# Stage 4 of a four-stage transformer kernel: comparisons in two parts, turned tiles ahead of sparse rows, weight roundings on other engines and steps

## The chip, the cores and the metric

The kernel runs on one core of a Trainium2 chip. The metric is the device time of one execution in microseconds (us), the median of the runs shown. In the profile PE is TensorE, PEld its weight loads, DVE VectorE, ACT ScalarE, POOL GpSimd and SP SyncE, which issues the DMAs. L686 is line 686 of the kernel. PSUM has eight banks of 512 float32 a partition.

## What is computed

Four residual blocks on x (2 x 1024 rows of 512, float32): each adds the layer norm of a block applied to the layer norm of x. The blocks are a per-token attention over heads, a feed-forward with ternary weights, a causal attention with rotary positions, and the one that most of the change touches:

```
h = silu(x @ w_gate) * (x @ w_up)          # 512 -> 2048
g = h.reshape(B, S, I // 4, 4)
_, idx = top_k(abs(g), 2)                  # of each four neighbours the two largest stay
h_sparse = g where kept, else 0
x = x + layernorm(h_sparse @ w_down)       # 2048 -> 512
```

## The kernel before

**Stages.** Stages 1 to 3 are the first three blocks. Stage 3 ends with `attention()`, a loop of 384 score units n on every engine: TensorE computes scores, ScalarE takes the exponential (L1349), GpSimd masks the diagonal (L1703), TensorE weighs the values two steps later. Then 12 steps `project(step)` follow, which project the second batch's eight tiles: ScalarE makes the high half of a tile (`out_hi`, tile OT, L1166), VectorE the low half (`out_lo`, L686), TensorE multiplies; statistics go over VectorE, GpSimd (L1588, L1594) and ScalarE (`norm6`), and GpSimd adds the residual (`residual`).

**Stage 4.** The rows are taken in four blocks k of 512, and each block in 16 steps, so s runs from 0 to 63, k = s // 16. Step s makes 128 of the 2048 hidden columns, transposed: hidden on partitions, 512 rows along the free axis. The hidden columns are dealt out so that four steps (a group g = s // 4) hold the four neighbours among which two are kept; comparing is then elementwise between four tiles. All products are float32 made of three passes with a rounded high half (float32r) and the low half of each operand, so every operand has to be split: the high half is a rounding copy, the low half a subtraction.

**TensorE** (`gate_up`, L2065): for step s 12 matmuls for gate into one PSUM bank and 12 for up into the next; then `down4(q)` for one hidden tile q of the sparse result, by the list `quarters` (L436): q is taken 7 to 9 steps after it was made, none before step 8. Gate, up and the turned tiles share a ring of four banks (4 to 7): each takes the bank of the fourth one before it in the list `fours` (L2049 `wait4`). So up of step s needs the bank of up of step s - 2, freed by VectorE's product; at steps 14 and 15 of a block, where two turned tiles (`turn4`, L2055) stand ahead of gate and up, up needs that of step s - 1.

**ScalarE**, each step s, in this order: at s % 16 in 13 and 14 two normalizations of the next block's rows (`norm4`), at 14 and 15 the high halves of two turned tiles (`turn4`, tile xT4); silu of gate (tile sl, L1553); then `split_w` three times, the high halves of the weights of gate and up for step s + 3 and down for q = s - 4 (ws_g, ws_u, ws_d, L1166); then `absolute(s)` (L1491, tile ab from hm), which waits for VectorE's product. Only at s % 4 == 3 is the absolute row ahead of the three copies.

**GpSimd**, each step: the low halves of the same weights (L1588). When the fourth of a weight block of four is done, SP issues the DMA that overwrites its slot of `rw4` (1 MB, four slots, asked for about a group ahead). At s % 16 == 6 it makes the statistics of the block before and adds its output rows to xb, at 11 the statistics of the next block's rows.

**VectorE**, each step s, in this order:

```
if g >= 1 and s % 4 == 0: sparse(g - 1, 0)     # compare: six is_ge rows from ab4 into cm4
if k < 3 and s % 16 == 11: four stats(...)     # L702, L703, L692, of the next block's rows
if g >= 1 and s % 4 == 1: sparse(g - 1, 1)     # count: 8 additions on cm4, 4 masks on hm4
if g >= 1 and s % 4 == 2: sparse(g - 1, 2)     # 4 casts to HH4 (L1079), 4 subtractions
if k < 3 and s % 16 in (14, 15): two turn4     # low halves of turned tiles
gate_up(s)                                     # hm4 = PSUM up * silu, frees both banks
```

`sparse(g, 0)` waits for all four absolute rows of its group; `compare` has three instructions, of 1536, 1024 and 512 columns. `absolute` of the next group waits until they are done (semaphore cma). After step 63 `last_compare(part)` and `last_count(part)` treat the last group in two halves of 256 columns, and the down products of the last four hidden tiles follow tile by tile.

**Around attention's end.** At n = 363, 366, 369 and 372 ScalarE rounds the first four gate weights (`split_w("g", ...)`) behind its exponential, GpSimd subtracts at the same n. In `project`, steps 2, 4 and 6, both do so for the first three up weights, behind `out_hi` and `norm6` of the step.

## Time and profile before

| what | us |
| --- | --- |
| median of 3 runs | 1397.03 |
| lowest and highest | 1394.22, 1397.66 |
| the profiled execution's own time | 1397.03 |
| its span in the trace | 1395.3 |
| TensorE busy | 1329.8 |
| VectorE busy | 1038.5 |
| GpSimd busy | 694.1 |
| ScalarE busy | 666.0 |

The trace covers the span; 1.73 us of the execution lie around it. Times in a timeline count from the span's start. A row of a timeline merges neighbouring instructions of one kind: start, time they took together, engine, line, operation, tiles (written <- read), shapes, how many. A bracket at its end is the time for which the engine had been idle, with the instruction that ended the wait. Attention's last units run at about 800 to 820, the projection to 845, stage 4 from there to the end.

### The profile page before, as it was taken

What the parts mean: (1) busy time and instruction counts of PE and PEld (TensorE: products, weight loads), DVE (VectorE), ACT (ScalarE), POOL (GpSimd) and SP (SyncE); (2) the same over time, 40 slices, a digit from 0 to 9 for tenths busy, and PEclk for the clock granted to TensorE, in tenths of its full rate; (3) what the DMA queues carried; (4) which work ended last, traced back from release to release, by engine and by line L of the source; (5) the groups of instructions that cost most, each with busy time, mean ns of one, the idle gap of its engine ahead of it and who ended that gap; (6) DMA issues with size and microseconds to landing.
All of it is one profiled execution on the core that took longest, in us unless ns stands there. A gap on an engine that the chain in (4) does not pass through costs nothing.

```text
span 1395.3 us, 19463 instructions
## 1 busy us (share of the span) xinstructions
PE 1329.8 (95%) x7206; PEld 912.9 (65%) x7206; DVE 1038.5 (74%) x1959; ACT 666.0 (48%) x1153; POOL 694.1 (50%) x836
## 2 busy tenths in 40 slices
PE   6989999999999899999999999998999999999997
PEld 5875446556455454555555467787888788878886
DVE  5898575665857758677666443998889878988897
ACT  6664342232325545455555575445454544454442
POOL 2576241421313413332433366776678768866863
PEclk9999999999999999999999999999999999999999
DMA  9100210204113213123013223122323422322300
GB/s 334 74 1 1 76 61 16 91 1 121 53 46 99 77 25 85 49 70 119 24 54 90 86 92 151 62 98 95 115 86 134 151 108 87 134 112 91 121 31 30
DMA packets 46270, 116.86 MB, mean 84 GB/s; under 512 B 3420, under 2 KB 4448, under 8 KB 42336
## 3 DMA queue, kind: packets, MB, share of 16 engines
q1 hardware_dynamic: 45104, 114.31, 24.0%
q8 instruction: 57, 0.93, 0.3%
q10 hardware_dynamic: 1072, 1.31, 0.3%
q14 instruction: 37, 0.30, 0.1%
HBM read 92.28 MB, written 23.07 MB: 83 GB/s over the span
## 4 chain that ended last, share of the span: by engine, by line
PE 61%; DVE 26%; ACT 5%; POOL 4%; issue 3%; DMA 1%; POOLq 0%; DVEq 0%; ACTq 0%
PE PS L1784 59%; DVE cm L686 7%; DVE SM L702 2%; DVE PS L919 2%; DVE HH L686 2%; DVE hm L695 2%; PE PS L1793 2%; DVE hm L686 1%; DMA rw<-in_L_ffn_w_up 1%; DVE HH L1079 1%; ACT EX L1349 1%; POOL SM L1588 1%; DVE HHx L1079 1%; DVE SM L698 1%; POOL ws_u L1588 1%
## 5 line engine op out<-in xcount | busy, mean ns | idle before, releaser
L1349 ACT ACTIVATE EX<-PS 128x512 f32<-128x512 f32 (+3 forms) x384 | 170.3, 494 | 134.4 <-PE PS L1784 132.6
L1588 POOL TENSOR_TENSOR SM<-SM 128x1 f32<-128x1 f32 x128 | 84.6, 661 | 214.4 <-DVE SM L692 210.6
L919 DVE CUSTOM_DVE_ANT_0 PS<-PS,MW 128x128 f32<-128x128 f32 (+3 forms) x256 | 122.5, 504 | 62.9 <-PE PS L1784 62.6
L1588 POOL TENSOR_TENSOR ws_g<-rw,ws_g 128x512 fp32r<-128x512 f32 x64 | 113.9, 1780 | 92.8 <-ACT ws_g L1166 92.8
L1784 PE MATMUL PS<-KG,QG 96*128 96x512 f32 (+3 forms) x384 | 134.8, 381 | 17.4 <-DVE SM L919 7.5
L1703 POOL TENSOR_SCALAR_AFFINE_SELECT EX<-EX 128x128 f32<-128x128 f32 x256 | 74.7, 302 | 149.0 <-ACT EX L1349 146.5
L1588 POOL TENSOR_TENSOR ws_u<-rw,ws_u 128x512 fp32r<-128x512 f32 x64 | 125.7, 1964 | 34.1 <-ACT ws_u L1166 34.1
L1784 PE MATMUL PS<-QG,KG 98*128 98x512 f32 (+3 forms) x384 | 131.3, 376 | 3.1 <-ACT EX L1349 2.7
L1784 PE MATMUL PS<-ws_d,HH 128*128 128x512 f32 x528 | 125.8, 389 | 0.9 <-DVE HH L686 0.8
L686 DVE TENSOR_TENSOR cm<-cm 128x512 bf16<-128x512 bf16 (+1 forms) x136 | 124.8, 948 | 2.4
L1784 PEld LDWEIGHTS PS<-QG,KG 98*128 98x128 f32 x384 | 69.6, 190 | 71.9 <-issue 45.6
L698 DVE TENSOR_REDUCE SM<-PS 128x1 f32<-128x512 f32 x128 | 87.7, 685 | 36.4 <-PE PS L1784 36.2
L1784 PEld LDWEIGHTS PS<-ws_d,HH 128*128 128x128 f32 x528 | 98.9, 188 | 22.2 <-issue 1.2
L1588 POOL TENSOR_TENSOR ws_d<-rw,ws_d 128x512 fp32r<-128x512 f32 x64 | 101.0, 1579 | 14.3 <-ACT ws_d L1166 14.3
L1784 PEld LDWEIGHTS PS<-KG,QG 96*128 96x128 f32 x384 | 72.2, 190 | 49.9 <-DVE SM L919 20.0
L686 DVE TENSOR_TENSOR cm<-ab 128x512 bf16<-128x512 f32 (+4 forms) x51 | 95.6, 1927 | 11.2 <-ACT ab L1491 11.2
L1784 PE MATMUL PS<-xT4a,ws_u 128*128 128x512 f32 x384 | 94.1, 395 | 4.9 <-DVE hm L686 4.8
L1491 ACT ACTIVATE ab<-hm 128x512 f32<-128x512 f32 x64 | 40.4, 632 | 120.9 <-DVE hm L686 120.9
L1784 PE MATMUL PS<-xT4b,ws_u 128*128 128x512 f32 x384 | 92.5, 390 | 0.8 <-DVE hm L686 0.7
L1784 PE MATMUL PS<-xT4a,ws_g 128*128 128x512 f32 x384 | 92.7, 390 | 0.0
L1784 PE MATMUL PS<-xT4b,ws_g 128*128 128x512 f32 x384 | 92.5, 390 | 0.0
L1166 ACT ACTIVATE ws_u<-rw 128x512 fp32r<-128x512 f32 x64 | 72.2, 1128 | 41.3 <-DMA rw<-in_L_ffn_w_up 41.3
(203 smaller groups left out, 2825.5 us busy)
## 6 DMA issues: line engine op xcount, KB each, us to landing
rw<-in_L_ffn_w_gate SPq DMA_DIRECT2D x16, 1024.0 KB, 5.1
rw<-in_L_ffn_w_up SPq DMA_DIRECT2D x16, 1024.0 KB, 7.1
rw<-in_L_ffn_w_down SPq DMA_DIRECT2D x16, 1024.0 KB, 7.9
QG<-qs SPq DMA_DIRECT2D x48, 256.0 KB, 4.2
raw<-in_L_ffn_w SPq DMA_DIRECT2D x3, 2816.0 KB, 11.6
qs<-stg SPq DMA_DIRECT2D x16, 512.0 KB, 3.5
xA<-xs SPq DMA_DIRECT2D x2, 2048.0 KB, 7.8
ys<-xA SPq DMA_DIRECT2D x4, 1024.0 KB, 4.2
```

Of the source, the lines that this page charges most:

```text
L686: return e.tensor_tensor(out, a, b, op)
L695: return e.scalar_tensor_tensor(out=out, in0=a, scalar=s, in1=b, op0=op0, op1=op1)
L698: return e.tensor_reduce(out, a, AX.X, op)
L702: w.wait_ge(S["dvs"], did(e.bn_stats(st, src)))
L919: last = e.tensor_tensor_reduce(out=p, in0=p, in1=MW[:, 512 - k1 + k0:512], scale=1.0, scalar=BIG, op0=ALU.add, op1=ALU.max, accum_out=m1)
L1079: n = did(e.tensor_copy(sparse4(q, 0), h[:, r, :]))
L1166: return e.activation(out, in_, ACT.Copy, scale=scale, bias=0.0)
L1349: e.activation(EX[:, n % 16, 0:W], PS[:, score_bank(n), 0:W], ACT.Exp, scale=ISQ, bias=0.0).then_inc(S["ex"], 1)
L1491: e.activation(ab4[:, s % 4, :], hm4[:, s // 4 % 2, s % 4, :], ACT.Abs, scale=1.0, bias=0.0).then_inc(S["ab"], 1)
L1588: return e.tensor_tensor(out, a, b, op)
L1703: e.affine_select(out=p, in_=p, compare_op=ALU.is_ge, fill=0.0, base=0, pattern=[[1, 128]], channel_multiplier=-1).then_inc(S["sel"], 1)
L1784: return e.matmul(out, l, r, start=start, stop=stop, skip_group_check=free)
```

## The change

It has five edits.

1. `compare` becomes `compare_three` (three of the six comparisons, those among the first three tiles; two instructions of 1024 and 512 columns) and `compare_last` (those with the fourth tile, one of 1536). `compare_three` of group g runs as `sparse(g, -1)` at s % 4 == 3, ahead of that step's product, and waits for three absolute rows; `compare_last` stays at s % 4 == 0. `last_compare` has only `compare_last` in it. `count` reads the rows in their new order.
2. VectorE makes the low halves of the turned tiles ahead of casts and subtractions, and the four statistics of step 11 two at step 11 and two at step 12 (GpSimd's likewise).
3. ScalarE's `absolute(s)` stands right behind silu in every step.
4. The high halves of the first four gate weights are made by VectorE (`gate_hi`, a `tensor_copy`), at the same n of its own order.
5. The third up weight is split at step 8 of the projection, on ScalarE and GpSimd.

```diff
+            def gate_hi(s):
+                q = raw_no[("g", 0)]
+                w.wait_ge(S["d_r%d" % (q % 4)], 16 * (q // 4 + 1))
+                w.wait_ge(S["st"], 336)
+                src = rw4[:, slot_r(q), :].rearrange("p (c g r) -> p r c g", c=4, r=4)[:, s]
+                e.tensor_copy(ws_g[:, s, 0, :].rearrange("p (c g) -> p c g", c=4), src).then_inc(S["hg"], 1)
...
+                    if n in (363, 366, 369, 372):
+                        gate_hi((n - 363) // 3)
...
-            def compare(a, cm, W):
-                tt(cm[:, 0:3, :], a[:, 0:1, :].broadcast_to([128, 3, W]), a[:, 1:4, :], ALU.is_ge)
-                tt(cm[:, 3:5, :], a[:, 1:2, :].broadcast_to([128, 2, W]), a[:, 2:4, :], ALU.is_ge)
-                return tt(cm[:, 5, :], a[:, 2, :], a[:, 3, :], ALU.is_ge)
+            def compare_three(a, cm, W):
+                tt(cm[:, 0:2, :], a[:, 0:1, :].broadcast_to([128, 2, W]), a[:, 1:3, :], ALU.is_ge)
+                return tt(cm[:, 2, :], a[:, 1, :], a[:, 2, :], ALU.is_ge)
+            def compare_last(a, cm, W):
+                return tt(cm[:, 3:6, :], a[:, 0:3, :], a[:, 3:4, :].broadcast_to([128, 3, W]), ALU.is_ge)
...
+                if phase == -1:
+                    w.wait_ge(S["ab"], 4 * g + 3)
+                    w.wait_ge(S["ey"], 16)
+                    compare_three(ab4, cm4, 512)
                 if phase == 0:
                     w.wait_ge(S["ab"], 4 * g + 4)
-                    w.wait_ge(S["ey"], 16)
-                    compare(ab4, cm4, 512).then_inc(S["cma"], 1)
+                    compare_last(ab4, cm4, 512).then_inc(S["cma"], 1)
...
-                if k < 3 and s % 16 == 11:
-                    for i in range(4):
+                if k < 3 and s % 16 in (11, 12):
+                    for i in range(2 * (s % 16) - 22, 2 * (s % 16) - 20):
...
-                if g >= 1 and s % 4 == 2:
-                    sparse(g - 1, 2)
                 if k < 3 and s % 16 in (14, 15):
                     i = 4 * (k + 1) + 2 * (s % 16 - 14)
                     turn4(i)
                     turn4(i + 1)
+                if g >= 1 and s % 4 == 2:
+                    sparse(g - 1, 2)
+                if s % 4 == 3:
+                    sparse(g, -1)
                 gate_up(s)
...
-                w.wait_ge(S["dvs"], did(compare(ab4[:, :, cols], cm4[:, :, cols], 256)))
+                w.wait_ge(S["dvs"], did(compare_last(ab4[:, :, cols], cm4[:, :, cols], 256)))
...
-                    if n in (363, 366, 369, 372):
-                        w.wait_ge(S["st"], 336)
-                        split_w("g", (n - 363) // 3)
...
-                if step in (2, 4, 6):
-                    split_w("u", step // 2 - 1)
+                if step in (2, 4, 8):
+                    split_w("u", (2, 4, 8).index(step))
...
-                if s % 4 == 3:
-                    absolute(s)
+                absolute(s)
                 if s > 0:
                     split_w("g", s + 3)
                 split_w("u", s + 3)
                 split_w("d", s - 4)
-                if s % 4 != 3:
-                    absolute(s)
```

## Rows read from the trace of the kernel before

**Rows 1.** The page's first part: busy time, share of the span, instructions, by engine.

```profile
PE 1329.8 (95%) x7206; PEld 912.9 (65%) x7206; DVE 1038.5 (74%) x1959; ACT 666.0 (48%) x1153; POOL 694.1 (50%) x836
```

**Rows 2.** TensorE's timeline: start, us, instructions; in brackets the gap and its end.

```profile
842.20 2.97 PE L1784 MATMUL PS<-CW,OT 128*128 128x512 f32 x12 [1.19 <-DVE OT L686]
...
888.41 4.49 PE L1784 MATMUL PS<-xT4a,ws_u 128*128 128x512 f32 x12 [2.44 <-DVE hm L686]
...
950.75 2.98 PE L1784 MATMUL PS<-xT4a,ws_u 128*128 128x512 f32 x12 [2.36 <-DVE hm L686]
...
958.29 1.22 PE L1793 MATMUL PS<-idf,sl 128*128 128x128 f32 x8 [1.84 <-DVE xT4b L695]
...
1092.13 0.63 PE L1793 MATMUL PS<-idf,sl 128*128 128x128 f32 x4 [0.76 <-DVE xT4a L695]
...
1227.30 1.23 PE L1793 MATMUL PS<-idf,sl 128*128 128x128 f32 x8 [1.88 <-DVE xT4b L695]
...
1377.17 11.58 PE L1784 MATMUL PS<-ws_d,HH 128*128 128x512 f32 x48 [0.79 <-DVE HH L686]
```

**Rows 3.** Windows view: stretch, its length, busy time of five engines, granted clock, DMA.

```profile
888.00:890.00 2.00, 1.59 (x4) 1.33 (x5) 2.00 (x6) 1.70 (x3) 0.00 (x0) 0.55 0.00 0
```

**Rows 4.** Timelines of TensorE, ScalarE and VectorE at attention's end.

```profile
814.47 0.39 PE L1784 MATMUL PS<-QG,KG 98*128 98x256 f32 x1 [1.00 <-ACT EX L1349]
...
812.86 1.18 ACT L1166 ACTIVATE ws_g<-rw 128x512 fp32r<-128x512 f32 x1
...
818.17 0.69 DVE L686 TENSOR_TENSOR OT<-OO,OT 128x512 fp32r<-128x512 f32 x1 [14.28 <-ACT OT L1166]
```

**Rows 5.** Timelines of VectorE and GpSimd where both want the memory, twice.

```profile
1190.29 1.42 DVE L1079 CAST HH<-hm 128x512 fp32r<-128x512 f32 x4
...
1191.63 2.48 DVE L686 TENSOR_TENSOR HH<-hm,HH 128x512 fp32r<-128x512 f32 x4
...
1191.48 4.07 POOL L1588 TENSOR_TENSOR ws_u<-rw,ws_u 128x512 fp32r<-128x512 f32 x1 [4.07 <-ACT ws_u L1166]
...
1222.81 3.74 DVE L686 TENSOR_TENSOR HH<-hm,HH 128x512 fp32r<-128x512 f32 x2
...
1224.28 1.73 POOL L1588 TENSOR_TENSOR ws_d<-rw,ws_d 128x512 fp32r<-128x512 f32 x1
```

**Rows 6.** ScalarE's timeline before the last projected tile.

```profile
839.71 1.10 ACT L1166 ACTIVATE ws_u<-rw 128x512 fp32r<-128x512 f32 x1
...
840.71 0.62 ACT L1166 ACTIVATE OT<-OO 128x512 fp32r<-128x512 f32 x1
```

**Rows 7.** VectorE's timeline, first group of stage 4.

```profile
866.97 0.69 DVE L686 TENSOR_TENSOR hm<-PS,sl 128x512 f32<-128x512 f32 x1 [4.75 <-PE PS L1784]
...
868.36 6.22 DVE L686 TENSOR_TENSOR cm<-ab 128x1536 bf16<-128x1536 f32 x3 [0.70 <-ACT ab L1491]
...
875.11 7.60 DVE L686 TENSOR_TENSOR cm<-cm 128x512 bf16<-128x512 bf16 x8
...
887.59 0.68 DVE L686 TENSOR_TENSOR hm<-PS,sl 128x512 f32<-128x512 f32 x1
```

**Rows 8.** ScalarE's timeline around the turned tiles of step 14.

```profile
950.64 0.63 ACT L1491 ACTIVATE ab<-hm 128x512 f32<-128x512 f32 x1 [0.62 <-DVE hm L686]
...
953.07 0.58 ACT L1166 ACTIVATE xT4b<-PS 128x512 fp32r<-128x512 f32 x1
...
954.02 1.14 ACT L1166 ACTIVATE ws_g<-rw 128x512 fp32r<-128x512 f32 x1
...
956.09 0.61 ACT L1166 ACTIVATE ws_d<-rw 128x512 fp32r<-128x512 f32 x1
```

**Rows 9.** VectorE's timeline: gated products of steps 23, 28 and 29.

```profile
1034.88 0.69 DVE L686 TENSOR_TENSOR hm<-PS,sl 128x512 f32<-128x512 f32 x1 [3.04 <-ACT sl L1553]
...
1071.10 0.69 DVE L686 TENSOR_TENSOR hm<-PS,sl 128x512 f32<-128x512 f32 x1 [0.90 <-PE PS L1784]
...
1084.82 0.68 DVE L686 TENSOR_TENSOR hm<-PS,sl 128x512 f32<-128x512 f32 x1
```

More of the change, by code:

```diff
@@ L1040, in turn4 @@
                 split_lo(bank4("t", t), xT4[k % 2][:, 0, :, sl], xT4[k % 2][:, 1, :, sl], 1.0, "xT4")
-            def compare(a, cm, W):
-                tt(cm[:, 0:3, :], a[:, 0:1, :].broadcast_to([128, 3, W]), a[:, 1:4, :], ALU.is_ge)
-                tt(cm[:, 3:5, :], a[:, 1:2, :].broadcast_to([128, 2, W]), a[:, 2:4, :], ALU.is_ge)
-                return tt(cm[:, 5, :], a[:, 2, :], a[:, 3, :], ALU.is_ge)
+            def compare_three(a, cm, W):
[3 more added lines that the diff above has]
+                return tt(cm[:, 3:6, :], a[:, 0:3, :], a[:, 3:4, :].broadcast_to([128, 3, W]), ALU.is_ge)
             def count(cm, h):
-                c01, c02, c03, c12, c13, c23, s0 = (cm[:, n, :] for n in range(7))
+                c01, c02, c12, c03, c13, c23, s0 = (cm[:, n, :] for n in range(7))
                 w.wait_ge(S["dvs"], did(tt(s0, c01, c02, ALU.add)))
@@ L1752, in pool_program @@
                 project(step)
-                if step in (2, 4, 6):
-                    split_w("u", step // 2 - 1)
+                if step in (2, 4, 8):
+                    split_w("u", (2, 4, 8).index(step))
             for s in range(64):
                 k = s // 16
-                if k < 3 and s % 16 == 11:
-                    for i in range(4):
+                if k < 3 and s % 16 in (11, 12):
+                    for i in range(2 * (s % 16) - 22, 2 * (s % 16) - 20):
                         n = 4 * (k + 1) + i
```

## The prediction

> **What bounds the kernel now.** The page's first part comes first: TensorE is busy 95% of the span, VectorE 74% [rows 1]. Little but TensorE's own gaps can be saved. So the next view is TensorE's timeline, where only the instructions that began after a gap count: in stage 4 and just before it there are gaps of 1.19, 2.44, 2.36, 1.84, 0.76, 1.88 and 0.79 us [rows 2], 11.3 us together, in 553 us. After the 2.44 us gap the windows view shows a mean granted clock of 0.55 for 2 us [rows 3]; the twelve products there took 4.49 us where the others took 2.97 [rows 2], 1.5 us more. What ended each gap: VectorE's gated product (hm, gate_up) or its low halves of turned tiles (xT4). So before 960 us VectorE's order of work sets the time, afterwards TensorE's own work does, but for a few gaps.
>
> **The change, part by part.** The profiled execution took 1397.03 us in all, 1.73 over its span; it is also the median of the three runs, so the sum starts there. This kernel's runs tell a change from none at about 0.3%, 4.2 us.
>
> *Gate weights at attention's end.* ScalarE gives up four copies of 1.18 us, which lie between its exponentials, and TensorE waits once, 1.00 us, for an exponential there [rows 4]. The copies gone, that gap goes. Nothing more: TensorE is otherwise without a gap in that stretch. VectorE takes the copies. It had nothing for 14.28 us until 818.17 [rows 4]; in its order the copies stand around the last tile statistics and ahead of out_lo(1, 0), which waits for ScalarE until 818. Bounds for one copy: 0.36 us, a free cast of the same size (1.42 for four), to that and a whole GpSimd instruction of 1.73 waited for [rows 5], 2.1. Four cost 1.4 to 8.4 us, all inside the 14.28; without that cover out_lo(1, 0) and the first projected tile would wait for them. GpSimd's low halves start earlier, so its masks aren't later. The Trainium skill ("GPSIMD Engine Reference", Specifications) says that GpSimd shares its SBUF interface with VectorE where VectorE copies in a 2-port mode or has two SBUF inputs; by that rule the copies would take the upper end. The sum is the same by either. Term: -1.0.
>
> *Third up weight at step 8.* In step 6 ScalarE copies ws_u for 1.10 us ahead of the high half of the last projected tile (OT, 840.71), and TensorE waits 1.19 us for the low half of that tile [rows 6, 2]. The move takes the copy out: OT starts 1.0 earlier, the gap shrinks to 0.2. On GpSimd the low half moves behind one residual; u(2) is needed two gated steps into stage 4, over 10 us after it will be there. Term: -1.0.
>
> *Parted comparisons.* Before, group 0's comparisons start when all four absolute rows are there: VectorE is idle 4.75 us ahead of the product at 866.97, compares from 868.36 for 6.22, counts from 875.11, and reaches the product at 887.59, for which TensorE has waited [rows 7, 2]. Three of six comparisons now run in that idle time. They cost between 1.9 us (three times a free subtraction of the same size, 2.48 / 4 [rows 5]) and 3.1 (half of 6.22 [rows 7], GpSimd being busy then), and the idle time holds either. The count starts at once when the next product, bound to TensorE, is done, about 2 us earlier (875.11 to about 873 on the old scale). So of 2.44 us of gap 2.0 go, and perhaps the 1.5 us of slow clock, which I leave to the range. Bounds 0 to 3.9 (2.44 + 1.5). Term: -2.0. In later groups the halves only change places: two waits for an absolute row (0.70 each [rows 7]) where one was, in time that VectorE has over. At the very end last_compare loses half of its columns twice; those chains end in HH, which ended TensorE's last gap of 0.79 [rows 2]. It gains 0 to 3, and I take the end near that gap. Term: -1.0.
>
> *Turned tiles ahead of sparse rows.* At steps 14 VectorE made casts and subtractions first and the low halves of the turned tiles behind them; TensorE waited 1.84, 0.76 and 1.88 us [rows 2]. These 4.5 us go. In their place VectorE now waits for ScalarE. ScalarE's absolute row of step 13 started at 950.64 and the second high half at 953.07 [rows 8]; now three weight copies stand in between (954.02 to 956.70 [rows 8], 2.7 us), so the high half ends 6 us after VectorE's product of step 13, not 3. Casts and subtractions, four and four, take 3.9 us unhindered (1.42 and 2.48, 1190.29 to 1194.11 [rows 5]); with the low half ahead and the product behind, 0.7 each, step 14's product ends some 11.3 us behind step 13's. TensorE would want it after three products of twelve and the tiles: 9.5 (950.75 to 958.29 without the gap are 5.7, one more is 2.8, the tiles about 1 [rows 2]). Where VectorE is already late, 1.8 us are given back, and 2.5 more if GpSimd hinders it (3.74 for two subtractions against half of 2.48 [rows 5]); where it is on time, none. Bounds: 0 to 12.9 for three times. I take 1.0 each, as GpSimd has mostly made its three low halves by then. Term: -4.5 + 3.0 = -1.5.
>
> *Absolute row always ahead of the weight copies.* This is the edit with a price that no row shows. ScalarE now waits for VectorE's product before it rounds the next weights, in three steps of four. What is queued behind: three copies (2.7 us), then silu of the next step, and GpSimd's three low halves and the DMAs that SP issues once those are done. The weights have three steps of slack (over 20 us), so they aren't late themselves. But GpSimd and VectorE hinder each other: a low half asked for amid a row of casts waited (4.07 us for one instruction, VectorE's four subtractions free, 2.48); in the other place VectorE's two subtractions took 3.74, two GpSimd instructions let in between [rows 5]. It depends on who comes first. Now each phase of VectorE meets just three low halves, which come 1.7 us after its product; mostly VectorE is then in mid-row. I take +0.5 in all, nearest to the first pair (bounds -1 to 13: no low half met, or rival C); the other end is the third rival.
>
> Sum: -1.0 - 1.0 - 2.0 - 1.0 - 1.5 + 0.5 = -6.0: **1391.0 us**.
>
> **Rivals.** *A, all of it (faster still).* VectorE keeps ahead of GpSimd in every row of casts. Then the gap of 2.36 us, which my sum leaves, goes too, and the 3.0 and 0.5 aren't paid: 1391.0 - 5.9 = 1385. For it: the free row at 1191.63 [rows 5]. Against: VectorE is busy nearly without a break from 868 to 958, so it isn't sure to catch up.
>
> *B, only the front.* The two 1.0 us gaps go, and stage 4 gives as much as it gets, since its bound there is VectorE with GpSimd behind the same memory interface, and no work of theirs is removed: 1395. This is also where the change doesn't do what it says, if the exponentials were late for another reason than the copies.
>
> *C, slower: statistics of output rows at steps 22 and 38.* GpSimd must now make three low halves (up to 1.73 each [rows 5]) between the product of step 22 and the statistics, which ScalarE waits for with its normalizations and, behind them, the silu of step 23. Before, those low halves were done by then, and VectorE still waited 3.04 us for that silu [rows 9]. Three low halves later it waits up to 5.2 more. GpSimd then has these, four additions and the next steps' low halves in a heap against VectorE's counts. Before, VectorE was on time again at step 28 with 0.90 us over, and the product of step 29 came at 1084.82 [rows 9], just as TensorE wanted it (ring of four banks, two of them taken by the turned tiles, so that step 30's product waits for step 29's). Step 29 then comes later by 5.2, less the 0.90 spare and up to 2.0 by which VectorE may be ahead: 2.3 at least; with two hindered pairs of subtractions (2.5 more each) in phases that were free, 7.3. From 0 on all of it is a gap in TensorE. Price: 5 us at each of two such places, 0.8 more there for turned tiles that now meet a late VectorE (1.8 instead of 1.0), 1 at the end, where step 54 has it but no tiles follow, less the 0.5 already counted: 1391.0 + 12.1 = 1403.1. For it: the hindered pair at 1222.81 [rows 5]. Against: comparisons and half the statistics move to lighter steps, and in the old order ScalarE also stood for a DMA there.
>
> **How the numbers follow.** Forecast 0.42; A 0.13; B 0.13; C 0.32. The forecast's own range is 1386 to 1396 (the tiles' term by 3, the compare and end terms by 2); of its 0.42, 0.31 lie more than 4.2 us below 1397, 0.11 within. So faster 0.31 + 0.13 = 0.44, same 0.11 + 0.13 = 0.24, slower 0.32. The range must hold A's middle and C's: 1384 to 1405, where A's far part and C's worst (7.3 us twice) are left out, under 2 in 10.
>
> **What would show it.** Right: no gap at ScalarE's exponentials near 814 and one of 0.2 at the last projected tile; the product that began at 887.59 comes 3 to 4 us earlier (2.0 by the comparisons, the rest by the front) and TensorE's gap there is below 1 us; the waits for xT4 gone or below 0.5; VectorE idle for ScalarE's xT4 at steps 14. Wrong: a gap of several us at the product of steps 30 and 46, waiting for VectorE's hm, and VectorE waiting over 5 us for silu of step 23: then C. Gaps only shifted with an equal sum: B. A stage 4 as before with the 1.00 us gap still there would refute the first term.

## The result, and the profile after

The changed kernel takes 1380.16 us (median of 4 runs, 1379.57 to 1381.80), the kernel before 1396.09 us (4 runs beside them, 1394.22 to 1397.66): ratio 0.9888, 95% interval 0.9871 to 0.9905, so it is faster by 15.9 us. The forecast was 1391.0 in a range from 1384 to 1405: the direction was right, the size was not, and the time lies below the range. The profiled execution took 1379.57 us, 1.8 over its span of 1377.8.

The page's first part, after:

```profile
PE 1321.3 (96%) x7181; PEld 911.1 (66%) x7206; DVE 981.6 (71%) x1961; ACT 659.4 (48%) x1149; POOL 697.2 (51%) x836
```

VectorE is busy 57 us less than before [rows 1], though the change takes only small pieces of its work away and adds four copies. That is the first sign of what the prediction missed. TensorE's timeline from the last projected tile on has these gaps left, and no others above 0.2 us:

```profile
837.32 3.01 PE L1796 MATMUL PS<-CW,OT 128*128 128x512 f32 x12 [0.88 <-DVE OT L686]
...
948.54 3.00 PE L1796 MATMUL PS<-xT4a,ws_u 128*128 128x512 f32 x12 [0.31 <-DVE hm L686]
...
1082.27 2.98 PE L1796 MATMUL PS<-xT4b,ws_u 128*128 128x512 f32 x12 [0.95 <-DVE hm L686]
...
1215.96 3.01 PE L1796 MATMUL PS<-xT4a,ws_u 128*128 128x512 f32 x12 [0.96 <-DVE hm L686]
```

Three gaps, 2.2 us, stand in stage 4 where the kernel before had six of 0.76 us and more [rows 2]. They are the up products of steps 15, 31 and 47, which wait for VectorE's gated product of the step before.

Group 0 on VectorE and, last, GpSimd's first low half behind it, to be laid beside [rows 7]:

```profile
863.52 1.76 DVE L686 TENSOR_TENSOR cm<-ab 128x1536 bf16<-128x1536 f32 x1 [0.70 <-ACT ab L1507]
867.57 0.69 DVE L686 TENSOR_TENSOR hm<-PS,sl 128x512 f32<-128x512 f32 x1 [2.29 <-PE PS L1796]
868.18 6.84 DVE L686 TENSOR_TENSOR cm<-cm 128x512 bf16<-128x512 bf16 x8
875.05 2.49 DVE L695 SCALAR_TENSOR_TENSOR hm<-cm,hm 128x512 f32<-128x512 bf16 x4
877.46 0.68 DVE L686 TENSOR_TENSOR hm<-PS,sl 128x512 f32<-128x512 f32 x1
878.07 1.42 DVE L1096 CAST HH<-hm 128x512 fp32r<-128x512 f32 x4
879.40 2.48 DVE L686 TENSOR_TENSOR HH<-hm,HH 128x512 fp32r<-128x512 f32 x4
...
879.93 3.38 POOL L1600 TENSOR_TENSOR ws_g<-rw,ws_g 128x512 fp32r<-128x512 f32 x1 [5.20 <-ACT ws_g L1186]
```

The same row of the kernel before, with GpSimd's low halves in it:

```profile
888.19 1.42 DVE L1079 CAST HH<-hm 128x512 fp32r<-128x512 f32 x4
889.53 5.29 DVE L686 TENSOR_TENSOR HH<-hm,HH 128x512 fp32r<-128x512 f32 x4
...
890.54 1.77 POOL L1588 TENSOR_TENSOR ws_g<-rw,ws_g 128x512 fp32r<-128x512 f32 x1 [3.43 <-ACT ws_g L1166]
892.26 1.99 POOL L1588 TENSOR_TENSOR ws_u<-rw,ws_u 128x512 fp32r<-128x512 f32 x1
894.21 1.75 POOL L1588 TENSOR_TENSOR ws_d<-rw,ws_d 128x512 fp32r<-128x512 f32 x1
```

Four subtractions took 5.29 us there and 2.48 here. I call such a row *free* when its four casts and four subtractions take 3.8 us, and *broken* when they take longer. After the change it is GpSimd that waits: asked for at 879.93, the low half takes 3.38 us instead of some 1.5 and ends at 883.31, 1.4 us behind VectorE's last subtraction. The groups by form say that this is no single case. Each line has the count, the group's busy time in us and, after the comma, the mean of one in ns. Before, from 838 to 1378 us:

```profile
L686 DVE TENSOR_TENSOR cm<-cm 128x512 bf16<-128x512 bf16 x120 | 118.7, 1019 | 2.1
L695 DVE SCALAR_TENSOR_TENSOR hm<-cm,hm 128x512 f32<-128x512 bf16 x60 | 61.5, 1085 | 0.5
L686 DVE TENSOR_TENSOR HH<-hm,HH 128x512 fp32r<-128x512 f32 x40 | 44.7, 1166 | 0.0
L1079 DVE CAST HH<-hm 128x512 fp32r<-128x512 f32 x40 | 24.6, 665 | 0.0
```

After:

```profile
L686 DVE TENSOR_TENSOR cm<-cm 128x512 bf16<-128x512 bf16 x120 | 121.1, 1039 | 2.1
L695 DVE SCALAR_TENSOR_TENSOR hm<-cm,hm 128x512 f32<-128x512 bf16 x60 | 48.7, 873 | 0.5
L686 DVE TENSOR_TENSOR hm<-PS,sl 128x512 f32<-128x512 f32 x64 | 43.9, 686 | 74.8 <-ACT sl L1569 41.3 <-PE PS L1796 32.8
L686 DVE TENSOR_TENSOR HH<-hm,HH 128x512 fp32r<-128x512 f32 x40 | 25.3, 681 | 0.0
L1096 DVE CAST HH<-hm 128x512 fp32r<-128x512 f32 x40 | 14.6, 417 | 0.0
```

Subtractions fell from 1166 to 681 ns, casts from 665 to 417, masks from 1085 to 873; with the 20 casts and 20 subtractions that write HHx that makes 58 us. The count (cm<-cm, 1019 and 1039 ns) is as slow as it was.

**Where the time came from.** A measure is needed that leaves out what happens ahead of the change. I take *stage 4's length*: span less the start of the last projected tile. It is 1395.3 - 842.20 = 553.1 before and 1377.8 - 837.32 = 540.5 after, 12.6 less. The last projected tile itself comes 4.9 us earlier, but 3.1 of these are not the change's: in the first profile of before the granted clock was 0.96 between 520 and 600 us, in a second one (below) 1.00, and there the tile comes at 839.08. So 1.8 us are the front's, 12.6 stage 4's, 3.1 that profile's dip of the clock: together the 17.5 us between the two spans. Such dips come with either kernel: a second profile of the changed one has 0.91 between 520 and 540 us, and its tile comes at 839.81.

### The profile page after: what moved, and what is told of

Read it like the earlier page. It is cut to its first block, busy times and chain, and to the rows that moved or that the text cites. A ratio compares the mean times of both kernels' runs of the same rounds, so it can differ in the third digit from the quotient of the medians.

```text
span 1377.8 us, 19437 instructions
## 1 busy us (share of the span) xinstructions
PE 1321.3 (96%) x7181; PEld 911.1 (66%) x7206; DVE 981.6 (71%) x1961; ACT 659.4 (48%) x1149; POOL 697.2 (51%) x836
## 4 chain that ended last, share of the span: by engine, by line
PE 78%; DVE 14%; ACT 4%; issue 2%; POOL 1%; DMA 0%; SPq 0%; POOLq 0%; DVEq 0%; ACTq 0%
PE PS L1796 76%; DVE PS L919 2%; DVE SM L702 2%; PE PS L1805 1%; DVE cm L686 1%; DVE hm L695 1%; DVE SM L698 1%; ACT EX L1369 1%; DVE qb L692 1%; DVE SM L703 1%; DVE tm L686 0%; DVE qa L692 0%; DVE xT L695 0%; DVE SM L692 0%; DVE hm L686 0%
## 5 line engine op out<-in xcount | busy, mean ns | idle before, releaser
L1600 POOL TENSOR_TENSOR ws_g<-rw,ws_g 128x512 fp32r<-128x512 f32 x64 | 134.5, 2102 | 117.5 <-ACT ws_g L1186 117.5
L686 DVE TENSOR_TENSOR cm<-cm 128x512 bf16<-128x512 bf16 (+1 forms) x136 | 128.3, 973 | 2.4
L1600 POOL TENSOR_TENSOR ws_u<-rw,ws_u 128x512 fp32r<-128x512 f32 x64 | 109.9, 1717 | 3.1 <-ACT ws_u L1186 3.1
L686 DVE TENSOR_TENSOR cm<-ab 128x1024 bf16<-128x1024 f32 (+3 forms) x49 | 88.7, 1836 | 16.1 <-ACT ab L1507 16.1
L686 DVE TENSOR_TENSOR hm<-PS,sl 128x512 f32<-128x512 f32 x64 | 43.9, 686 | 74.8 <-ACT sl L1569 41.3
```

Source lines behind the costliest of these rows:

```text
L686: return e.tensor_tensor(out, a, b, op)
L1600: return e.tensor_tensor(out, a, b, op)
```

## Experiments

All times are medians in us, "length" is stage 4's length in the run's profile. The kernels ran in four groups, with the kernel before in each: its medians were 1400.1, 1397.0, 1397.3 and 1396.4, its single runs lay between 1392.0 and 1405.9, the changed kernel's between 1379.6 and 1386.9. So the ratios tell each kernel from the one before, but hardly variants of the changed kernel from each other: with the absolute row back the ratio is 0.9893, and the changed kernel has 0.9888 and 0.9893. Between variants I go by the length and by the gaps that make it up.

| kernel | time | ratio to before, 95% | length |
|---|---|---|---|
| before, two profiles | 1396.1 to 1400.1 | 1 | 553.1, 559.6 |
| changed, two profiles | 1380.2, 1381.2 | 0.9888 (0.9871 to 0.9905), 0.9893 (0.9867 to 0.9919) | 540.5, 540.5 |
| changed, absolute row back | 1385.2 | 0.9893 (0.9869 to 0.9916) | 545.2 |
| before, absolute row alone | 1384.1 | 0.9890 (0.9863 to 0.9918) | 542.0 |
| changed, comparisons whole | 1382.9 | 0.9881 (0.9854 to 0.9909) | 543.1 |
| changed, tiles behind | 1382.9 | 0.9881 (0.9856 to 0.9905) | 543.9 |
| before, comparisons parted alone | 1390.7 | 0.9948 (0.9928 to 0.9967) | 548.1 |
| before, tiles ahead alone | 1408.6 | 1.0081 (1.0060 to 1.0103) | 565.7 |
| changed, absolute row in the middle | 1382.3 | 0.9885 (0.9865 to 0.9906) | 541.8 |
| before, front alone | 1393.2 | 0.9961 (0.9943 to 0.9979) | 549.9 |
| changed, statistics whole | 1382.9 | 0.9894 (0.9871 to 0.9917) | 542.6 |
| before, short low halves | 1378.8 | 0.9865 (0.9839 to 0.9891) | 537.2 |
| before, absolute row and tiles | 1386.6 | 0.9932 (0.9909 to 0.9955) | 546.7 |
| changed, high halves first, twice | 1378.2, 1378.7 | 0.9857 (0.9827 to 0.9887), 0.9866 (0.9838 to 0.9893) | 537.5, 537.2 |

**The absolute row put back.** In ScalarE's loop of the changed kernel:

```
-                absolute(s)
+                if s % 4 == 3:
+                    absolute(s)
                 ...
+                if s % 4 != 3:
+                    absolute(s)
```

> The changed kernel with one edit undone: in ScalarE's steps the absolute row stands behind the three weight copies again, but for every fourth step. Theory 1 (the place of the absolute row frees VectorE: with it, each row of casts, subtractions and masks is no longer broken by GpSimd's low halves): 5 to 10 us slower than the changed kernel's 1380.2, so 1385 to 1390; the mean of VectorE's 40 subtractions HH<-hm goes from 0.68 us back to 1.1 or more, the casts from 0.42 to 0.6 or more, VectorE's busy time in stage 4 rises by 40 us or more, and TensorE again waits for hm(5) near 880 us. Theory 2 (the order of VectorE's own work, parted comparisons and turned tiles, brought the gain; the absolute row is worth about nothing, as the prediction's +0.5 had it): within 2 us of 1380.2, whatever the means are.

Measured 1385.2, length 545.2: 4.7 more, and TensorE's gaps of 0.2 us and more in stage 4 add up to 6.6 us against 2.2. Subtractions are at 959 ns (1100 or more had been expected), casts at 735, masks at 1261, VectorE busy 428.7 us in stage 4 against 408.6; TensorE waits 0.93 us for VectorE's product of step 5 (at 881.62) and 2.58 for that of step 14. The busy time rose by 20 us, not by the 40 expected, since count and comparisons got shorter (count 911 ns instead of 1039). Theory 1 holds in time and in kind, its sizes don't; theory 2 (within 2 us) fails.

**The absolute row alone**, the same lines on the kernel before.

> The kernel before with one edit alone: the absolute row always ahead of the weight copies. Theory 1: 5 to 10 us faster than before (1386 to 1391), VectorE's subtractions HH<-hm at 0.7 us in the mean, the casts at 0.42; the 2.44 us gap at the product of step 5 smaller by more than 1 us, but gaps for the low halves of turned tiles still there. Theory 2: within 2 us of 1396. Theory 3 (the edit pays only together with turned tiles ahead, since turned tiles behind a sparse row meet a VectorE that waits later for ScalarE): slower than before or within 2 us, with lower means all the same.

1384.1 us, below the 1386 to 1391 of theory 1, length 542.0: 11.1 less than the shorter of the two lengths of before, nearly all of what the whole change brings. Its groups:

```profile
L695 DVE SCALAR_TENSOR_TENSOR hm<-cm,hm 128x512 f32<-128x512 bf16 x60 | 39.4, 718 | 0.5
L686 DVE TENSOR_TENSOR HH<-hm,HH 128x512 fp32r<-128x512 f32 x40 | 26.4, 712 | 0.0
L1079 DVE CAST HH<-hm 128x512 fp32r<-128x512 f32 x40 | 14.6, 419 | 0.0
```

The expected gaps for turned tiles did not stay: with a VectorE on time, tiles behind the sparse row cost 0.2 us each. What took their place is a gap of another kind, 1.54 us at 886.79, where the gate weights' low half is late from GpSimd.

**Comparisons whole again, tiles behind again**, each on the changed kernel (compare in one phase at each group's first step and at the end; VectorE's `turn4` behind `sparse(g - 1, 2)`).

> The changed kernel with all six comparisons in one phase again, at each group's first step and at the end for each half of the columns. Theory 1: the parting was worth about what the prediction gave it, 1 to 3 us (1381 to 1383): a gap of 0.5 to 2 us at the product of step 5 near 880 us and one below 1 us at the last products. Theory 2: the parting is the larger part of the gain, 4 to 8 us slower (1384 to 1388).

> The changed kernel with VectorE's low halves of turned tiles behind the sparse rows again, at steps 14, 30 and 46. Theory 1: the unhindered casts and subtractions (3.9 us for eight) would let the low halves come early enough for TensorE or nearly so; 0 to 3 us slower (1380 to 1383), with gaps for xT4 below 1 us each and the 0.95 us gaps at the products of steps 30 and 46 gone. Theory 2: gaps of 1.8 us and more for xT4 at the three places, 4 to 6 us slower (1384 to 1386).

Both 1382.9; lengths 2.6 and 3.4 more. Theory 1 has the time of both, but not the places. The first has its gap not at VectorE's product, as expected, but at GpSimd's low half, and one of 0.71 at the last products; the second has two gaps for turned tiles of the size that theory 2 named:

```profile
885.47 3.01 PE L1787 MATMUL PS<-xT4a,ws_g 128*128 128x512 f32 x12 [1.57 <-POOL ws_g L1591]
```

```profile
1078.63 1.23 PE L1805 MATMUL PS<-idf,sl 128*128 128x128 f32 x8 [2.18 <-DVE xT4a L695]
...
1213.54 1.23 PE L1805 MATMUL PS<-idf,sl 128*128 128x128 f32 x8 [2.20 <-DVE xT4b L695]
```

**The kernel before, once more**, for its profile alone.

> The kernel before itself, for a second profile of it. If the slower clock that its first profile shows between 520 and 600 us is chance and not of the kernel, the granted clock there is 1.00, the last projected tile comes at 838.8 instead of 842.2, and the span is about 1391.9 (1395.3 less 3.4); stage 4 has the same gaps (2.44, 2.36, 1.84, 0.76, 1.88, 0.70, 0.79, each within 0.3), and again a granted clock below 0.7 after the first of them. If the clock is of the kernel, the span is 1395 again.

The clock between 520 and 600 us was 1.00, so the dip comes and goes. But the span was 1398.7: the expected 1391.9 failed, for a reason that matters. The up product of step 30 had no gap in the first profile (I had found VectorE just in time there, with 0.90 us over [rows 9]); here it waits 3.92 us, and the clock falls to its lower level behind it:

```profile
1087.67 5.27 PE L1784 MATMUL PS<-xT4b,ws_u 128*128 128x512 f32 x12 [3.92 <-DVE hm L686]
```

```profile
1088.00:1092.00 4.00, 4.00 (x10) 3.11 (x10) 4.00 (x7) 4.00 (x8) 1.79 (x2) 0.50 0.01 2
```

So the kernel before has no one length. Its rows break differently from one execution to the next: the one behind the product of step 25 took 3.8 us in the first profile (from 1056.0) and 10.1 in the second (from 1053.1), and VectorE, but for 0.70 us without a pause from there on, has the product of step 29 at 1086.85 (1084.82 in the first, less 3.1 on this scale), for which step 30's up product waits. The two lengths differ by 6.5 us, and its runs spread over 14. The single profile that I predicted from had the shorter stage 4 of the two.

**Comparisons parted alone; tiles ahead alone.** The two edits of VectorE's order, each by itself on the kernel before.

> The kernel before with the parted comparisons alone (and the order of the six rows that they need). Theory 1 (the edits remove the same lateness of VectorE, each as much as it shortens VectorE's row ahead of a late product): the 2.44 us gap at the product of step 5 shrinks by 2 to 2.44 us and the slow clock behind it goes (1.5 us), the 0.79 gap at the end goes, the 2.36 us gap at step 15 and those for xT4 stay: 4 to 6 us faster than a profile of before at full clock, span 1386 to 1388 against 1391.9. Theory 4 (VectorE's order alone settles the phase, the same freeing of its rows as with the absolute row): 8 us or more, span 1384 or less, and subtractions below 0.9 us in the mean.

> The kernel before with the turned tiles ahead of the sparse rows alone. Theory 1: the gaps for xT4 (1.84, 0.99, 1.88) go; in their place gaps of 1 to 2.5 us at the products of steps 14, 30 and 46, which wait for VectorE's hm; 0 to 3 us faster, span 1389 to 1392. The prediction's own terms say -4.5 + 3.0. Rival: the gap at step 15 of 2.36 goes as well, 5 us or more faster, span 1387 or less.

The parting alone: 1390.7, length 5.0 less, within theory 1's 4 to 6. But 0.89 us are left of the 2.44, where it allowed 0.44, and the subtractions are at 903 ns, close to theory 4's limit of 0.9 us: the parting moved the phase a little, too. The tiles alone: 1408.6, 11 us *slower* than the kernel before. Neither theory had that. TensorE's and VectorE's timelines show it:

```profile
959.65 4.28 PE L1784 MATMUL PS<-xT4a,ws_u 128*128 128x512 f32 x12 [2.63 <-DVE hm L686]
...
1100.34 4.87 PE L1784 MATMUL PS<-xT4b,ws_u 128*128 128x512 f32 x12 [4.72 <-DVE hm L686]
...
1241.13 4.48 PE L1784 MATMUL PS<-xT4a,ws_u 128*128 128x512 f32 x12 [4.71 <-DVE hm L686]
...
1090.22 0.69 DVE L695 SCALAR_TENSOR_TENSOR xT4a<-PS,xT4a 128x512 fp32r<-128x512 f32 x1 [5.43 <-ACT xT4a L1166]
...
1092.01 1.42 DVE L1079 CAST HH<-hm 128x512 fp32r<-128x512 f32 x4
1093.35 6.24 DVE L686 TENSOR_TENSOR HH<-hm,HH 128x512 fp32r<-128x512 f32 x4
```

VectorE waits 5.43 us for ScalarE's high half, and the row behind it, pushed later, meets all three low halves: 6.24 us for four subtractions. The next up product waits 4.72 us, and each product behind such a gap runs in part at the lower clock (4.28 to 4.87 us for twelve matmuls, else 3.0). The gaps at the three products are 12.1 us together, close to the upper bound that the prediction named for them (12.9); the lower clock behind them costs 4.6 us more, for which it had no term.

**The absolute row in the middle**, behind the gate weights' copy, on the changed kernel.

> The changed kernel with ScalarE's absolute row one place further back: behind the copy of the gate weights, ahead of those of the up and down weights. If what matters is that no low half of GpSimd is under way or queued when VectorE begins a row (it begins right behind its product, the gate copy's low half would be there by then), then the subtractions and casts are hindered again, at least half as much as in the kernel with the absolute row last (0.96 and 0.74 us in the mean there, 0.68 and 0.42 in the changed one): means above 0.8 and 0.55, VectorE busy 10 us or more above the changed kernel's 408.6 in stage 4, 1 to 4 us slower than it. If it matters only that the heap of three copies isn't ahead, the means stay within 5% of the changed kernel's and the time within 1 us of it.

1382.3, length 541.8, 1.3 more; subtractions at 773 ns, casts at 482, VectorE busy 9 us more, just short of the first theory's numbers (0.8, 0.55 and 10), well above the second's. Ten of its first 14 rows stay free.

**The front alone; the statistics whole.** The two edits ahead of stage 4 on the kernel before; all four statistics of new rows in step 11 on the changed kernel.

> The kernel before with the two edits ahead of stage 4 alone (gate weights' high halves made by VectorE, the third up weight at step 8). What the prediction said: the gap of 1.00 us for the exponential goes, the one at the last projected tile shrinks (to 0.2 by the prediction, 0.88 by the changed kernel's trace): 1.3 to 2 us faster than a profile of before in the same state of stage 4, that is a span of 1390 to 1391 if step 30's product has no gap (1391.9 less these), 1397 if it has one of 4 us, as in the second profile of before. Rival B (the front gives, stage 4 takes it back): no gap near 811 us, stage 4 begins 1.3 to 2 us earlier and the span is 1392 or more with no gap of 4 us at step 30.

> The changed kernel with the four statistics of new rows all in step 11 of each block again, and none in step 12. Theory 1 (VectorE has time over in these steps now that its rows are free): within 1 us of the changed kernel's 1380.2. Rival (two more statistics, 2.0 us, push the product of step 11 or the comparisons behind it past TensorE's need, as in the kernel before with its late product of step 30): 2 to 5 us slower, with a gap at a product of steps 12, 13 or 14.

The front: the 1.00 us gap is gone, the last projected tile has 0.89 us, and the time is 4.1 us below the median of before beside it. The tile's start shows 1.8 of that. The ratio's interval means 2.9 to 8.0 us, so there is more; its profile has a stage 4 of 549.9, with no gap at step 30's product and 6 of 14 rows free. Whether the front's edits bring that or chance does is not shown. Rival B, by which stage 4 takes the gain back, isn't seen. The statistics: 2.1 us longer (gap at step 15 of 0.95 instead of 0.31, count at 1150 ns instead of 1039), more than theory 1's 1 us. The split seems to have a worth of its own, for which the prediction had no term.

**Short low halves**: the kernel before, GpSimd's low halves an eighth of their columns, seven eighths left out. This asks for the cause directly.

```
+                if s >= slots and kind == "d":
+                    lo, src, hi = lo[:, 0:64], src[:, 0:64], hi[:, 0:64]
+                elif s >= slots:
+                    lo, src, hi = lo[:, :, 0:16], src[:, :, 0:16], hi[:, :, 0:16]
                 tt(lo, src, hi, ALU.subtract).then_inc(S["w" + kind], 1)
```

> The kernel before, but GpSimd makes the low halves of the weights after the first four or five of each kind for an eighth of the columns only and the rest is left out; every order, wait and DMA stays. Theory 1 (VectorE is late in the kernel before because GpSimd's low halves break its rows): VectorE's subtractions at 0.7 us in the mean instead of 1.17, casts 0.42 instead of 0.67, masks 0.65 instead of 1.08; none of the gaps for the products (2.44, 2.36, 3.92) above 1 us, those for xT4 of 1.8 us mostly gone, too; span 1380 to 1384. Theory 2 (VectorE is late by its own order of work): the means fall, but the gaps stay above 1.5 us each and the span at 1388 or more.

```profile
L686 DVE TENSOR_TENSOR cm<-cm 128x512 bf16<-128x512 bf16 x120 | 50.5, 451 | 2.0
L695 DVE SCALAR_TENSOR_TENSOR hm<-cm,hm 128x512 f32<-128x512 bf16 x60 | 38.7, 707 | 0.5
L686 DVE TENSOR_TENSOR HH<-hm,HH 128x512 fp32r<-128x512 f32 x40 | 26.1, 701 | 0.0
L1079 DVE CAST HH<-hm 128x512 fp32r<-128x512 f32 x40 | 15.0, 425 | 0.0
```

1378.8 us (span 1375.6, below the 1380 to 1384 expected) with every order of the kernel before: no gap of 0.2 us or more between the last projected tile and the end, VectorE busy 303.5 us in stage 4 instead of 469.9. Its own order of work made nothing late; GpSimd beside it did. Theory 2 is out. The edit shortens GpSimd's own chain as well, but in the kernel before each of the six larger gaps ended with an instruction of VectorE's [rows 2], none with a low half.

**Which rows break.** Taken from the timelines of 14 of the profiles (all but the short one's and the repeats of the changed kernel and of high halves first, below), the first 14 rows of casts and subtractions of each, 196 in all, by where GpSimd's low halves stand to the row's start. The fifteenth is left out: in ten profiles VectorE waits for TensorE in the middle of it (0.2 to 2.8 us), and it takes 5.2 to 6.8 us.

| low half | rows free (3.8 us) | rows broken (4.3 to 10.1 us) |
|---|---|---|
| under way at the row's start | 0 | 51 |
| none under way, first asked before 1.15 us | 1 | 14 |
| first asked 1.15 to 2.30 us into it | 101 | 3 |
| first asked later | 12 | 2 |
| none in it | 12 | 0 |

In the kernel before 3 of its 14 rows were free, in the changed one and in the absolute row alone 14 of 14. There the low half is always asked for 1.87 us into the row (or none is): from VectorE's product it is 0.72 us to the absolute row's start (877.46 to 878.18), 0.54 to the gate copy's, 1.21 to the low half's (879.93), less 0.61 from the product's start to the row's. In the kernel before one was still under way at the start of 10 of its 14 rows. The table is no full rule. Three rows broke though the low half was asked for at the same 1.87 us: two in the kernel with tiles behind again, which are its gaps of 2.18 and 2.20, one in that with the absolute row in the middle. And group 0's row of the kernel before, shown above, is one of the two broken in the fourth line: nothing was under way, and the low half was asked for 2.35 us into it. What tells these five from the other 113 of the two lines is open.

**Absolute row and tiles together; high halves first.** It was open why the tiles' edit loses alone and gains in the changed kernel. The first of these has just the two edits on the kernel before. The second is meant to beat both kernels: on the changed kernel ScalarE makes the high halves of step 14's turned tiles in step 13, ahead of its absolute row:

```
                 e.activation(row4("s", s), PS[:, bank4("g", s), :], ACT.Silu, scale=1.0, bias=0.0).then_inc(S["si"], 1)
+                if k < 3 and s % 16 == 13:
+                    turn4(4 * (k + 1))
+                    turn4(4 * (k + 1) + 1)
                 absolute(s)
```

> The kernel before with two edits: absolute row always first, turned tiles ahead of the sparse rows. If the absolute row's place alone turns the tiles' edit round, its rows of casts and subtractions are all free (3.8 us), the gaps at the up product behind steps 14, 30 and 46 are 1 us or less each, and the time is within 2 us of the absolute row alone (1384.1), not above it by more. If the tiles' edit needs the parted comparisons too, it is 1387 or more, with gaps of 2 us and more there.

> The changed kernel with ScalarE's high halves of the first two turned tiles (those of step 14) moved from the start of step 14, where they stand behind the absolute row and three weight copies of step 13, to step 13, ahead of its absolute row. TensorE has turned them some 2 us before VectorE's product of step 13, so ScalarE has them when VectorE comes. If the three gaps left in the changed kernel (0.31, 0.95 and 0.96 us at the products of steps 14, 30 and 46) are VectorE's wait of 4.4 us for these high halves, they go and nothing takes their place: 2.2 us faster than 1380.2, 1378.0, span 1375.6. Rival: the absolute row and with it the weights' low halves come later and break VectorE's rows again: same or slower, with subtractions above 0.75 us in the mean.

> The changed kernel itself, beside the two below: 1380.2 within 1 us; its profile shows the same three gaps of 0.31, 0.95 and 0.96 us in stage 4 and rows of casts and subtractions of 3.8 us.

> The changed kernel with ScalarE's high halves of step 14's turned tiles ahead of step 13's absolute row, on the same chip and in the same call as the changed kernel: 2 to 3 us below it (the 2.2 us of gaps, all gone in its first profile), 1377.5 to 1378.5. If the first comparison was chance of the call: within 1 us of it.

Absolute row and tiles: 1386.6, all 14 rows free, gaps of 0.98, 0.96 and 0.98 us at the three products, length 546.7 against 542.0 without the tiles. So with free rows the tiles' edit loses 4.7 (2.5 by the medians) instead of 12.6 (6.1, if one takes the second profile of before), and it is a gain (3.4) beside the parted comparisons and the split statistics. Which of these two turns it round was not tried, and the gain leans on the two broken rows of the kernel with tiles behind, whose cause is open. The time fell between the two outcomes that I had written down (above 1386.1, below 1387).

High halves first: 1378.2 and, in one group with the changed kernel's 1381.2, 1378.7; the runs of the two don't overlap (1375.8 to 1379.3, 1379.6 to 1386.9). Its timelines of VectorE and, last, ScalarE at step 13 and 14:

```profile
1072.74 1.27 DVE L695 SCALAR_TENSOR_TENSOR xT4a<-PS,xT4a 128x512 fp32r<-128x512 f32 x2
1073.94 2.78 DVE L1096 CAST HH<-hm 128x512 fp32r<-128x512 f32 x4
1076.64 4.93 DVE L686 TENSOR_TENSOR HH<-hm,HH 128x512 fp32r<-128x512 f32 x4
...
1070.27 1.09 ACT L1186 ACTIVATE xT4a<-PS 128x512 fp32r<-128x512 f32 x2 [5.28 <-PE PS L1808]
1072.86 0.63 ACT L1507 ACTIVATE ab<-hm 128x512 f32<-128x512 f32 x1 [1.50 <-DVE hm L686]
```

The high halves fit into time in which ScalarE had nothing, the low halves follow VectorE's product at once, and though the row behind them is broken in all three places (subtractions 804 ns in the mean), as the rival said, no gap of 0.2 us is left in stage 4. Its lengths of 537.5 and 537.2 us are also that with short low halves (537.2): TensorE's own work.

## Why the prediction was right in direction and wrong in size

- **Gate weights at attention's end, -1.0: right.** The gap is gone, and VectorE's copies cost nothing: 1.18 and 1.75 us for two each, 2.9 in all where the bounds were 1.4 and 8.4, so not at the upper end that the rule cited there would give. VectorE still waits 10.02 us ahead of out_lo(1, 0).
- **Third up weight, -1.0: too much.** The gap went from 1.19 to 0.88. The low half that TensorE waits for took 1.37 us instead of 0.69, while GpSimd's addition of the residual ran beside it:

```profile
835.80 1.37 DVE L686 TENSOR_TENSOR OT<-OO,OT 128x512 fp32r<-128x512 f32 x1 [2.37 <-ACT OT L1186]
...
835.34 1.29 POOL L1600 TENSOR_TENSOR xA<-xA,yn 128x512 f32<-128x512 f32 x1 [0.90 <-ACT yn L1189]
```

- **Parted comparisons, -2.0 and -1.0 at the end: right in kind, and about in size.** 2.6 in the changed kernel, 5.0 alone, the 0.79 at the end included. The 1.5 us of lower clock that the prediction had left to its range are gone in the changed kernel, too. Group 0's count started 2.0 us earlier on stage 4's scale (868.18 against 875.11, less 4.9), as said. But VectorE's product behind it came 7.0 us earlier (877.46 against 887.59, less the 3.1 of the clock), not 3 to 4: masks of 2.49 instead of 4.92 us. Masks of 718 ns with the absolute row alone and 1083 with the parting alone (1085 before) say that this is the absolute row's work, not the comparisons'.
- **Turned tiles, -4.5 + 3.0: right in the changed kernel.** The tiles' gaps are gone, VectorE waits 4.42 us for ScalarE in their place, and the three products are late by 2.2 us together where I had 3.0. What I did not see is that the same edit, alone, stands near the other end of its bounds (12.1 of 0 to 12.9), with the lower clock on top, and loses: its sign hangs on the other edits.
- **Absolute row always ahead, +0.5: this is the step that failed**, "nearest to the first pair", with bounds of -1 and 13. It measured -11.1 alone and -4.7 among the others. The two cases were on the page, a free row where GpSimd waits 4.07 us and a pair broken to 3.74 [rows 5], and so was the choice between them: low halves "1.7 us after its product", VectorE mostly in mid-row. The trace agrees: 1.79 us after the product's end, 1.87 into the row, and 14 of 14 rows free. What failed is the price. I set the good case down as a small loss, as if the rows of before were in it, too, and never counted them: 11 of the 14 were broken. The lower bound of -1 held only "no low half met", not what the rows of before were already losing: 1166 ns in the mean for a subtraction that takes 620 when free (2.48 for four [rows 5]), and with casts and masks 58 us of VectorE's time. With them went most of the 2.36 us gap (0.31 is left), which the sum had left standing.
- **The statistics**: no term; 2.1 in length, less certain than the others (the gap at step 15 accounts for 0.6 of it).
- **The base.** The sum started from one profile and took its gaps for the kernel's. Two profiles of before differ by 6.5 us in stage 4, and the one that I had is the shorter; its dip of the clock, 3.1 us, was in the sum's start as well.

Rival A had the mechanism, VectorE ahead of GpSimd in every row, with a chance of 0.13. Against the profiled 1379.6 its 1385 is 5.4 too high: 3.1 of that is the dip of the clock in the base, 1.5 the lower clock behind the 2.44 us gap, which it left in; the rest isn't taken apart. Rival B did not occur. Rival C named a place that is real (step 30's product in the second profile of before waits 3.92 us), but the wrong kernel for it: VectorE's wait for the silu of step 23 rose from 3.04 to 5.43 us, the sign that the prediction had named for C. No gap of TensorE's followed; that the free rows behind it took the wait up fits, but is argued.

The edits are not additive. In length, alone on the first profile of before: absolute row -11.1, comparisons -5.0, tiles +12.6. The whole: -12.6.

## What to carry to other kernels

When two engines hold each other up, price an edit by the time from one engine's row to the other's first request, and work that time out from rows; then count in the trace of before how many passes are already in the bad case, since a good case is a gain only against those. One move that makes the time the same in every pass was worth more here than the cuts in VectorE's order. Test an edit of order with and without its neighbours: here one was 11 us worse alone and 3 us better in company. And take two profiles of a kernel with waits before a sum is made on one.

## What the runs showed of the hardware

- An engine that asks in the middle of the other's row waits to the row's end, not to that of one instruction: GpSimd's low half took 3.38 us where VectorE went on with its subtractions for 1.95 of them (879.93 to 881.88). One that is already under way breaks the row, in 51 of 51 cases, and then the two take turns (in the broken row shown above, three low halves of 1.77, 1.99 and 1.75 us stand beside four subtractions of 5.29). The Trainium skill ("SBUF — State Buffer", in its section on the two separate sides) says that the pair of ports that VectorE shares with GpSimd is an exclusive lock, taken by VectorE's instructions with two SBUF inputs or in a 2-port mode, and that whichever instruction starts first has it to its end. The 51 rows agree; that VectorE mostly keeps it over a row of several instructions is what the 101 free rows add, with the five exceptions above against it.
- VectorE's products with one operand in PSUM took 684 ns before and 686 after, its subtractions with both in SBUF 1166 and 681: of these two, only the latter are held up.
- The granted clock behind a gap of TensorE is not settled by its length alone: after gaps up to 2.07 us ahead of an up or gate product the next twelve matmuls took 3.0 us in every profile, after gaps of 2.36 to 2.83 us 2.98 to 3.00 in some and 4.28 to 4.57 in others (2.44 us: 4.49 in one profile of the kernel before, 2.98 in the other), after 3.92 us and more 4.48 to 5.27 always, with a granted clock of 0.50, the lower of the two levels (1.2 GHz).
